# Sums of q's squares for the q norm: from four TensorE products to VectorE turns and adds with one small product, in a cross-attention and expert-layer kernel

## The reference

```python
def attention(h, ctx, mask):             # 32 query heads of 128, 8 key/value heads
    q = (h @ Wq.T)  -> [b, 32, 64, 128];  k, v = ctx @ Wk.T, ctx @ Wv.T -> [b, 8, 64, 128]
    q = q * rsqrt(mean(q*q, -1) + EPS) * q_norm_w       # RMS norm of each row of a head
    k = the same with k_norm_w, repeated for 4 query heads each; v repeated too
    p = softmax(q @ k.T / sqrt(128) + mask)
    return (p @ v) as [b, 64, 4096] @ Wo.T

x = x + tanh(g_xattn) * attention(layernorm(x), ctx, mask)
x = x + tanh(g_ffn) * moe(layernorm(x))  # 16 experts (2 per row) of 128, a shared one of 512
```

## Time and profile before

| | |
|---|---|
| runs, median of 3 | 1417.54 us (1417.51 to 1418.62) |
| profiled execution, span | 1417.8 us |
| attention stage | from about 207 to 1100 us |
| PE busy | 1405.3 us (99%) |
| DVE busy | 850.8 us (60%) |
| ACT busy | 514.2 us (36%) |
| POOL busy | 359.5 us (25%) |
| granted TensorE clock | 9 tenths or more in all slices |

### The profile page before, as it was taken

One profiled execution on the slowest core, in us unless ns is written; L12 is line 12 of the kernel. 1 busy time (PEld: TensorE's weight loads), 2 busy tenths in 40 slices (PEclk: granted clock), 3 DMA queues, 4 the chain that ended last, 5 costly groups with the idle time before them and its releaser, 6 DMA issues.

```text
span 1417.8 us, 26787 instructions
## 1 busy us (share of the span) xinstructions
PE 1405.3 (99%) x9135; PEld 1124.3 (79%) x9136; DVE 850.8 (60%) x1807; ACT 514.2 (36%) x1117; POOL 359.5 (25%) x374
## 2 busy tenths in 40 slices
PE   9999999999999999999999999999999999999998
PEld 7888887778787787878787878787878888777777
DVE  6444447666666666666666666565678746243359
ACT  5333344333343334333333333333334331222242
POOL 1122223121212121211112121212122101366646
PEclk9999999999999999999999999999999999999999
DMA  7544331111111111111111111111123244554548
GB/s 224 180 124 141 126 116 42 38 35 38 42 37 34 38 41 39 34 37 41 39 33 43 38 41 31 47 32 42 45 79 97 97 149 164 192 194 163 162 149 297
DMA packets 91230, 125.48 MB, mean 89 GB/s; under 512 B 7184, under 2 KB 57360, under 8 KB 90896
## 3 DMA queue, kind: packets, MB, share of 16 engines
q1 hardware_dynamic: 83632, 99.70, 22.3%
q0 software_dynamic: 7520, 24.65, 5.2%
HBM read 86.84 MB, written 37.49 MB: 88 GB/s over the span
## 4 chain that ended last, share of the span: by engine, by line
PE 80%; DVE 2%; issue 1%; DMA 0%; ACT 0%; POOL 0%; DVEq 0%; ACTq 0%
PE ps L592 19%; PE ps L594 18%; PE ps L593 18%; PE ps L978 6%; PE ps L679 5%; PE ps L721 4%; PE ps L994 3%; PE ps L687 2%; PE ps L706 2%; PE ps L973 1%; DVE acc L1878 1%; DVE acc L1885 1%; PE ps L1025 1%; PE ps L891 1%; PE ps L729 0%
## 5 line engine op out<-in xcount | busy, mean ns | idle before, releaser
L489 POOL CAST vth<-vt 128x256 fp32r<-128x256 f32 x64 | 25.4, 396 | 629.6 <-PE ps L721 618.0
L1483 DVE TENSOR_TENSOR al<-ps,ah 128x256 fp32r<-128x256 f32 x256 | 96.0, 417 | 116.3 <-ACT ah L1165 116.3
L1165 ACT CAST ah<-ps 128x256 fp32r<-128x256 f32 x256 | 83.6, 384 | 194.8 <-PE ps L594 188.4
L1477 DVE TENSOR_TENSOR acc<-ps,acc 128x512 f32 (+1 forms) x128 | 87.9, 687 | 109.0 <-PE ps L594 109.0
L592 PE MATMUL ps<-hT,w0h 128*128 128x512 f32 (+1 forms) x384 | 152.2, 396 | 0.0
L594 PE MATMUL ps<-hT,w0h 128*128 128x512 f32 (+1 forms) x384 | 149.9, 390 | 0.0
L593 PE MATMUL ps<-hT,w0l 128*128 128x512 f32 (+1 forms) x384 | 149.5, 389 | 0.0
L483 POOL TENSOR_TENSOR qr<-qv,mhalf 128x8 f32<-128x8 f32 x64 | 105.1, 1642 | 83.4 <-DVE qv L1492 82.3
L1134 ACT COPY qs<-ps 128x512 f32<-128x512 f32 x128 | 75.2, 587 | 120.9 <-PE ps L594 120.9
L1143 ACT ACTIVATE pb<-pb 128x256 f32<-128x256 f32 x128 | 48.3, 418 | 166.3 <-DVE pb L1510 166.2
L592 PE MATMUL ps<-w0l,ah 128*128 128x512 f32 x256 | 103.0, 402 | 0.0
(11 more groups left out here) (238 smaller groups left out, 3079.0 us busy)
## 6 DMA issues: line engine op xcount, KB each, us to landing
wraw<-in_w_att SPq DMA_DIRECT2D x64, 256.0 KB, 2.6
vbuf<-vo SPq DMA_DIRECT2D x16, 512.0 KB, 3.3
kbuf<-ko SPq DMA_DIRECT2D x16, 512.0 KB, 3.8
kt<-kbuf SPq DMA_DIRECT2D x32, 256.0 KB, 2.9
vt<-vbuf SPq DMA_DIRECT2D x64, 128.0 KB, 2.0
wgu<-in_w_gu SPq DMA_DIRECT2D x4, 2048.0 KB, 8.1
y<-ybuf SPq DMA_DIRECT2D x16, 512.0 KB, 6.2
xt<-in_x SPq DMA_DIRECT2D x16, 256.0 KB, 4.0
```

Source lines behind the costliest of these rows:

```text
L1165: act.copy(ah[:, bp, :, b2, :], pv_view(bp, b2)).then_inc(a_hi, 1)
L1477: dve.tensor_tensor(dst, PS[6 + bp][:], dst, ALU.add).then_inc(acc_done, 1)
L1483: dve.tensor_tensor(al[:, bp, :, b2, :], pv_view(bp, b2), ah[:, bp, :, b2, :], ALU.subtract).then_inc(a_lo, 1)
```

## The change

The sums are split in two. VectorE turns each head's squares, 128 x 512, in blocks of 32 x 32 into sqT (`turn_squares`) and adds up the 32 numbers of each row of a block (`sum_squares`), so that sqs has, on 32 rows in each of the four groups of partitions, a quarter of each sum. One product of TensorE with the matrix fold (128 x 128, one where two partitions are the same modulo 32) adds the four quarters up and writes them to all four groups, 32 columns for two heads, two halves of rows and 8 batches. In the softmax the turn of bank 2 is gone; a product with the matrix quarter, which keeps in each group of partitions its own 8 of the 32 columns, and an add over the four now give qv.

`q_sums(r + 2)` moves on TensorE: it was behind the scores, and is now in the middle of the first output projection. It waits for VectorE's sums (sq_part) in place of ScalarE's squares (q_sq), and ScalarE writes new squares once VectorE has turned the old ones (sq_turned) in place of after the product (ss_done). The waits for ss_turned ahead of the scores in the opening are gone. On VectorE, `dve_step` turns head 0 first, adds up behind `probs_lo`, and takes head 1 behind `a_rest(i - 1, 0)`; the `slice_lo` of an even step is moved into the odd step that follows. In the last steps the new operations stand beside the residuals, and an extra wait for the squares stands ahead of `transpose_h2(2, 0)`. GpSimd no longer fills ones32; VectorE builds fold and quarter from the identity matrix in the key and value part.

```diff
             def q_sums(j):
-                pe.wait_ge(q_sq, 2 * j + 2)
-                for r in range(4):
-                    s0 = 32 * (r % 2)
-                    mm = pe.matmul(PS[2][32 * r:32 * r + 32, 0:256], ones32[:], sq[:, r // 2, :, s0:s0 + 32],
-                                   start=True, stop=True)
-                mm.then_inc(ss_done, 1)
+                pe.wait_ge(sq_part, 2 * j + 2)
+                pe.matmul(PS[2][:, 0:32], fold[:].rearrange("p a j -> p (a j)"), sqs[:].rearrange("p h r b -> p (h r b)"),
+                          start=True, stop=True).then_inc(ss_done, 1)
...
             def outputs(r, w_before, w_o, o_ready=None):
                 pe.wait_ge(acc_done, 2 * r + 1)
-                project_out(1, w_before, (0, 1, 2, 3))
+                project_out(1, w_before, (0, 1))
+                q_sums(r + 2)
+                project_out(1, w_before, (2, 3))
...
                 scores(d + odd, 1 - odd)
-                q_sums(i + 1)
                 if last:
+                    pe.wait_ge(q_sq, 2 * i + 4)
                     transpose_h2(2, 0)
...
-            pe.wait_ge(acc_zero, 2)
-            q_sums(0)
+            pe.wait_ge(fold_ok, 4)
             def opening():
 
                 for i in range(2):
                     for h in range(2):
                         pe.wait_ge(q_sq, 2 * i + 1 + h)
                         q_head(h, 1 - i, i, W[0]).then_inc(q_done, 1)
+                        if h == 0:
+                            q_sums(i)
                     pe.wait_ge(s_scaled, i + 1)
-                    pe.wait_ge(ss_turned, i + 1)
                     scores(i, 1 - i)
-                    q_sums(i + 1)
...
             def squares(h, j):
-                act.wait_ge(ss_done, j + 1)
+                act.wait_ge(sq_turned, 2 * j + 1 + h)
...
+            dve.wait_ge(ident_ok, 2)
+            dve.tensor_reduce(fold1[:], ident[:].rearrange("p (a j) -> p j a", a=4), AX, ALU.add).then_inc(fold_ok, 1)
+            dve.tensor_reduce(quarter[:], ident[:].rearrange("p (a j) -> p a j", a=4), AX,
+                              ALU.add).then_inc(fold_ok, 1)
+            dve.wait_ge(fold_ok, 2)
+            dve.tensor_copy(fold[:], fold1[:].unsqueeze(1).to_broadcast([P, 4, 32])).then_inc(fold_ok, 2)
...
+            def turn_squares(j, h):
+
+                if not isinstance(j, int) or 2 * j + h > 0:
+                    dve.wait_ge(sq_part, 2 * j + h)
+                dve.wait_ge(q_sq, 2 * j + 1 + h)
+                dve.transpose(sqT[:].rearrange("p n i -> p (n i)"), sq[:, h].rearrange("p b s -> p (b s)")).then_inc(
+                    sq_turned, 1)
+
+            def sum_squares(j, h):
+
+                dve.wait_ge(sq_turned, 2 * j + 3 + h)
+                dve.tensor_reduce(sqs[:, h].rearrange("p r b -> p b r"), sqT[:].rearrange("p (b r) i -> p b r i", r=2), AX, ALU.add).then_inc(sq_part, 1)
...
-                dve.transpose(sst[:].rearrange("p b r -> p (b r)"), PS[2][:, 0:256]).then_inc(ss_turned, 1)
+                dve.scalar_tensor_tensor(out=ssg[:].rearrange("p b q -> p q b"),
+                                         in0=PS[2][:, 0:32].rearrange("p (q b) -> p q b", q=4),
+                                         scalar=HD * EPS, in1=quarter[:].unsqueeze(2).to_broadcast([P, 4, 8]),
+                                         op0=ALU.add, op1=ALU.mult).then_inc(ss_turned, 1)
                 dve.wait_ge(ss_turned, j + 1)
-                dve.tensor_scalar(qv[:], sst[:, :, 0], HD * EPS, None, ALU.add).then_inc(q_var, 1)
+                dve.tensor_reduce(qv[:], ssg[:], AX, ALU.add).then_inc(q_var, 1)
...
                 i = 2 * d + odd
+                turn_squares(i + 1, 0)
                 if odd:
                     probs_lo(i, 1)
+                sum_squares(i + 1, 0)
+                if odd:
+                    slice_lo(i - 1, w, sl - 1)
                 if complete[0] is not None:
                     residual(complete[0], 1)
                 a_rest(i - 1, 0)
+                squares_summed(i + 1, 1)
                 if complete[1] is not None:
                     residual(complete[1], 0)
...
-                slice_lo(i, w, sl)
+                if odd:
+                    slice_lo(i, w, sl)
...
             def opening():
+                for h in range(2):
+                    squares_summed(1, h)
                 softmax(1, lambda: probs_lo(0, 0), lambda: None)
                 slice_lo(0, W[1], 0)
+                for h in range(2):
+                    squares_summed(2, h)
                 softmax(2, lambda: probs_lo(1, 1, 6), lambda: a_rest(0, 0))
...
             i = STEPS - 3
+            turn_squares(i + 1, 0)
             probs_lo(i, 1)
+            sum_squares(i + 1, 0)
+            slice_lo(i - 1, W[0], NC - 4)
             statistics(0)
             residual(5, 1)
+            squares_summed(i + 1, 1)
             a_rest(i - 1, 0)
...
             i = STEPS - 2
             h2T_rest(0, 2)
             h2T_rest(1, 3)
+            squares_summed(i + 1, 0)
             residual(7, 1)
+            squares_summed(i + 1, 1)
             a_rest(i - 1, 0)
```

More of the change, by code:

```diff
@@ L157, in build @@
             pb = sb("pb", [P, 8, S], F32, a)
-            sst = sb("sst", [P, 8, 32], F32, a)
+            ssg = sb("ssg", [P, 8, 4], F32, a)
+            sqs = sb("sqs", [P, 2, 2, 8], F32, a)
+            sb("below_vth", [P, 192], F32, a)
             v_hi = sb("vth", [P, 2, HD], F32R, a)
@@ L166, in build @@
             wraw = sb("wraw", [P, 512], F32, a)
-            ones32 = sb("ones32", [P, 32], F32, a)
             qv = sb("qv", [P, 8], F32, a)
@@ L211, in build @@
             g_hl = sb("g_hl", [P, KD, P], F32R, a)
+            sqT = sb("sqT", [P, 16, 32], F32, a)
         with ExitStack() as a:
@@ L220, in build @@
         rab = sb("rab", [P, NT, E], BF16)
+        fold1 = sb("fold1", [P, 32])
+        fold = sb("fold", [P, 4, 32])
+        quarter = sb("quarter", [P, 4])
         xt3 = (sgt[0], aft[0])
@@ L245, in build @@
         ss_turned, v_split, pT_hi = sem("ss_turned"), sem("v_split"), sem("pT_hi")
+        sq_turned, sq_part, fold_ok = sem("sq_turned"), sem("sq_part"), sem("fold_ok")
         pT_done, pT_evac, pv_done, a_hi, a_lo, o_done, acc_done = (
@@ L477, in _ @@
             pool.memset(accf[:, 4096:8192], 0.0).then_inc(acc_zero, 1)
-            pool.wait_ge(hT_lo, NT)
-            pool.memset(ones32[:], 1.0).then_inc(acc_zero, 1)
             def inverse_root(j):
@@ L807, in opening @@
                 q_head(0, 1, 1, W[0]).then_inc(q_done, 1)
+                q_sums(2)
                 probs_v(0, 0)
@@ L818, in opening @@
                 pe.wait_ge(s_scaled, 3)
-                pe.wait_ge(ss_turned, 3)
                 scores(1, 1)
-                q_sums(3)
                 pe.wait_ge(acc_done, 4)
@@ L1367, in _ @@
             dve.sem_inc(kn_done, 2)
+            dve.sem_inc(sq_turned, 2)
             dve.sem_inc(a_lo, 4)
@@ L1484, in a_rest, with squares_summed @@
                                       ALU.subtract).then_inc(a_lo, 1)
+            def turn_squares(j, h):
[7 more added lines that the diff above has]
+                dve.tensor_reduce(sqs[:, h].rearrange("p r b -> p b r"), sqT[:].rearrange("p (b r) i -> p b r i", r=2), AX, ALU.add).then_inc(sq_part, 1)
+            def squares_summed(j, h):
+                turn_squares(j, h)
+                sum_squares(j, h)
             def softmax(j, *meanwhile):
@@ L1565, in dve_step @@
                 softmax(i + 1, while_root, while_exp)
-                slice_lo(i, w, sl)
+                if odd:
+                    slice_lo(i, w, sl)
             rest_first(range(4, 8))
+            for h in range(2):
+                squares_summed(0, h)
             softmax(0)
@@ L1577, in opening @@
                 slice_lo(1, W[1], 1)
-                dve.wait_ge(acc_zero, 3)
+                dve.wait_ge(acc_zero, 2)
                 add_out(2, 0, 0)
```

## The result

The changed kernel takes 1429.85 us (median of 4, 1428.82 to 1430.80) against 1417.53 us: the ratio is 1.0081, with an interval of 1.0068 to 1.0095. It is slower, where 1418.0 was forecast.

What follows compares the result with a forecast made beforehand. The prediction took TensorE, busy 99% of 1417.8 us, as the bound. Pairs -11.1, opening +6.3 and last steps +5.3 sum to +0.5 on the 1417.54 median: 1418.0 us forecast, range 1411 to 1427.

Steps and rivals of the forecast that it cites:

- The 0.57 us of L687: On TensorE, the four small fp32 products that sum q's squares, eight instructions, would go: 0.57 us a step.
- The small product: On TensorE in the first output projection, the new fp32 summing product would cost 0.24 us, bounds 0.17 and 0.40.
- the rival of a dear product: Slower: the small product costs 0.40 us instead of 0.24 in each of 59 steps, giving 1427 us; chance 0.12.
- Turn and sum: On VectorE, turning a head's 128x512 squares takes about 0.71 us and adding them up 0.69.
- the rivals that moved them: Slower: turn and sum exceed 1.40 us, 1425 at 0.90 a turn, chance 0.24; faster: turn near 0.545, 1411, chance 0.22.
- The odd step's wait: In odd steps TensorE waits 0.15 us for VectorE's sums plus 0.10 for starting again, leaving a gain of 0.08.
- The last steps: From step 58 on, VectorE's added work beside the residuals makes TensorE wait: +5.3 us, bounds 3 to 8.
- the softmax's head in the even steps: Its chain begins later by half a projection, but its probabilities are needed only next step, so nobody waits: no cost.
- 0.4 of waiting: In even steps among the last, TensorE waits 0.4 us for the probabilities' rests, behind head 1's turn and sum on VectorE.
- An even step: In the undisturbed pairs the small product does not wait in an even step, so TensorE gains 0.33 us.
- The opening: Before the steps overlap, VectorE's turns and sums ahead of each softmax cost +6.3 us, bounds 3 and 8.
- the pairs: 27 undisturbed pairs of an even and an odd step, steps 4 to 57, gain 0.41 us each: -11.1 us.

Runs made afterwards that it cites:

- e1: The changed kernel with VectorE taking the turned probabilities' rests ahead of the softmax's head in the even steps; 1425.91 us, ratio 1.0050.
- e3: The changed kernel with another order in the opening alone: step 0's probability turns behind the next q product, a q copy ahead of exponentials; 1428.07 us.
- e4: The changed kernel with products that nobody reads in the opening's two long TensorE waits; 1426.43 us, ratio 1.0057.
- e5: The changed kernel with VectorE's outer loop over 16 steps written out three times; 1428.78 us, ratio 1.0071.
- e6: e2 with the old way of summing (products with ones, turn of the bank) for steps 0 to 2 and 59 to 63; 1405.66 us, ratio 0.9906.
- e8: e6 with VectorE's outer loop written out; 1403.67 us, ratio 0.9895.
- e2: e1 with the small product behind three heads of the first projection in place of two; 1417.94 us, ratio 0.9998.

## Why the prediction was wrong

**Right.** The 0.57 us of L687 are gone. The small product costs 0.23 where 0.24 was taken; the rival of a dear product fell. By the rule of the Trainium skill, "TensorE: Matmul & The Clock Gate", section "LDWEIGHTS (loading the stationary operand)", two loads of 128 columns would have been 0.21 alone (an estimate from its figure); the product with both loads is 0.14 from start to start, so the trace disagrees. Turn and sum are 0.704 and 0.686, forecast 0.71 and 0.69, so the rivals that moved them fell too. The odd step's wait is 0.17 and 0.10, forecast 0.15 and 0.10. The last steps lost 4.34 up to step 63 and 5.9 up to the expert layer, forecast 5.3.

**The step that failed**, worth 5 to 6 us: of the softmax's head in the even steps the prediction said that "that chain begins later by half a projection and ends in probabilities that are needed only in the next step, so nobody waits for it". The head's own result is not needed soon, but its instruction stands in VectorE's queue ahead of the turned probabilities' rests, and the second projection needs those. The new wait was followed on the engine that waits for the product, not through the queue behind it. The same order was seen for the last steps ("0.4 of waiting") and not carried over to the loop. An even step gained 0.14, not 0.33; in e1 it gains 0.35.

**The opening**, forecast +6.3 with 8 as the bound, was +10.05. The chain was 7.2 to 7.4 (e3, e4), about 1 more than worked out; 2.7 is the clock, which no term had. The earlier trace rows show a clock of 1.00 in two stretches in which TensorE was busy all the time; a sum that forecasts delays of 2 to 4 us in front of TensorE has to ask what the clock does behind them.

**The loops**, 2.5 us, were not in the sum. In the kernel before, VectorE's first operation at this place waited for ScalarE as it does in the earlier trace rows, and for as long as in nearly all other even steps (2.4 to 2.5 us):

```profile
548.26 0.68 DVE L1533 TENSOR_TENSOR w1l<-wraw,w1h 128x512 f32 x1
551.35 0.76 DVE L1483 TENSOR_TENSOR al<-ps,ah 128x256 fp32r<-128x256 f32 x2 [2.41 <-ACT ah L1165]
```

So a slow start of the loop would have had cover there, as e5's theory A says. But the traces do not show that there was one to cover. In the change an instruction transfer falls into each of the two slow starts (DMA view, 556.5 to 559.0 and 781.9 to 784.1; packets, MB, share):

```profile
q14 instruction: 1, 0.01, 1.5%
...
q14 instruction: 1, 0.01, 0.9%
```

With the loop written out (e5) none falls there. The kernel before has no transfer on this queue from 485 to 1040 us, and e6 none from 485 to 980. And e6, in which VectorE's loop returns to the same turn, starts it at once at the second return:

```profile
764.15 0.68 DVE L1589 TENSOR_TENSOR w1l<-wraw,w1h 128x512 f32 x1
764.75 0.70 DVE L1516 STREAM_TRANSPOSE sqT<-sq 128x512 f32<-128x512 f32 x1
```

So the slow start goes with the transfer, and not with a loop's return as such. The Trainium skill, "Runtime: NRT & Kernel Launch", section "Instruction fetch mechanics", has a rule for it: instructions are fetched ahead in sequence only, and a taken branch to a place outside the pages at hand stops the engine until they are fetched. The traces agree as far as they go: 2.48 and 2.15 us at the loop's returns with a transfer in each, and none of either with it written out (e5). Why the change's returns need a transfer and those of e6 and of the kernel before do not is not shown.

**The time around the span.** Each run of the two kernels lies 1.7 to 1.8 us above its span (1417.60 and 1415.8; 1429.59 and 1427.8). So the profiled execution of before, with a span of 1417.8, took about 1419.6 by this estimate, 2 us more than the median run; the prediction set span against time and took it as 0.3. This is why 10.0 us between the two spans are 12.3 between the medians. Much of it lies in the expert layer, which the change leaves alone: there the trace of before has five waits for acteT and that of the change one, of 0.5:

```profile
PE ps L994 <- DVE acteT L1849: 1.4, 5, 0.5
```

In e8 too the lag falls there, from -15.48 to -17.06. So the lag ahead of the expert layer, 12.76, is the better measure of what the change cost.

Together: +3.75 in the opening, +8.6 in the pairs and +0.6 in the last steps, less 0.7 of a start that was earlier, are the 12.3 that lie between +0.5 and +12.76.

## What to carry to other kernels

A wait that is added to an engine is paid by everything queued behind it there: go down that queue until an instruction that another engine needs within the wait's reach, and put that one ahead. Work that has room in the middle of a pipeline may have none at its two ends; the old way can stay there. The return of a loop can cost an engine over 2 us in one program and nothing in another: when a loop's body has changed, look at the first operation behind each return, and at the transfers of the kind instruction in the DMA view.

## What was not expected of the hardware

After 2.6 us in which TensorE stood, the granted clock went from 1.00 to 0.50 (1.2 GHz) at 223.6 us, although TensorE had begun to work again at 222.2. It stayed there for 3.4 us, in which large products took 0.43 us in place of 0.23; the second such stretch lasted 6.7 us in e2 and e5, with the same program there, and the opening lost about 1 us more there. VectorE took 2.48 and 2.15 us from the last operation of a loop body of 16 steps to its first one, where a written-out body took none (e5), and where the same loop took none in e6.
